# 64-wide attention of a fused two-layer kernel: the order of TensorE's work in slots 1, 4 and 12 of a round

## The reference, cut to what matters

```python
h = _rms(x, ln_w)
q = (h @ wq).reshape(B, S, NHEADS, HEAD_DIM)      # 32 heads of 64
k = (h @ wk).reshape(B, S, KVHEADS, HEAD_DIM)     # 8 groups
v = (h @ wv).reshape(B, S, KVHEADS, HEAD_DIM)
q, k = _rope(q, k)
scores = jnp.einsum('bqhd,bkhd->bhqk', q, k) / np.float32(np.sqrt(HEAD_DIM))
scores = jnp.where(causal[None, None], scores, jnp.float32(-1e+30))
attn = jax.nn.softmax(scores, -1)
o = jnp.einsum('bhqk,bkhd->bqhd', attn, v).reshape(B, S, NHEADS * HEAD_DIM)
x = x + o @ wo
```

## Time and profile before

| what | value |
|---|---|
| median of 3 runs | 2113.06 us (2111.1 to 2116.01) |
| the profiled execution, its own time | 2112.84 us |
| its span | 2111.0 us |
| mean granted TensorE clock | 0.935 of full speed |
| busy over the span | PE 86%, PEld 58%, DVE 63%, ACT 52%, POOL 43% |

### The profile page before, as it was taken

One profiled execution on the slowest core, in us unless ns is written; L12 is line 12 of the kernel. 1 busy time (PEld: TensorE's weight loads), 2 busy tenths in 40 slices (PEclk: granted clock), 3 DMA queues, 4 the chain that ended last, 5 costly groups with the idle time before them and its releaser, 6 DMA issues.

```text
span 2111.0 us, 32365 instructions
## 1 busy us (share of the span) xinstructions
PE 1810.6 (86%) x10666; PEld 1224.6 (58%) x10666; DVE 1320.8 (63%) x3898; ACT 1097.9 (52%) x2886; POOL 917.8 (43%) x1013
## 2 busy tenths in 40 slices
PE   4989899867888845999999999999999994799994
PEld 2656678733434323666666666666667664555552
DVE  5675545446686855777877777787777766522222
ACT  3323244226565533767666676666667661344441
POOL 3991000002221001555555555555555551588884
PEclk9999899958999986999999999999999995899997
DMA  5000020000001010000000000000000007255556
GB/s 152 1 1 2 1 60 1 1 0 1 1 1 41 1 43 1 1 1 1 1 1 1 1 1 1 1 1 1 1 1 1 1 1 276 73 82 84 82 84 163
DMA packets 61426, 61.71 MB, mean 29 GB/s; under 512 B 13136, under 2 KB 58320, under 8 KB 61264
## 3 DMA queue, kind: packets, MB, share of 16 engines
q0 software_dynamic: 15360, 20.98, 6.3%
q1 hardware_dynamic: 45904, 38.65, 5.7%
HBM read 40.48 MB, written 19.14 MB: 28 GB/s over the span
## 4 chain that ended last, share of the span: by engine, by line
PE 62%; DVE 21%; issue 8%; ACT 4%; POOL 3%; DMA 2%; SPq 0%; ACTq 0%; POOLq 0%; DVEq 0%
PE banks L1799 7%; PE banks L1818 6%; PE banks L1787 5%; PE banks L1777 5%; PE banks L1808 5%; DVE wide_x L1052 4%; PE banks L1995 3%; PE banks L1830 3%; PE banks L1621 3%; PE banks L1872 3%; PE banks L1847 2%; DVE con L1063 2%; POOL wdT L725 2%; PE banks L1683 2%; PE banks L1892 2%
## 5 line engine op out<-in xcount | busy, mean ns | idle before, releaser
L1777 PE MATMUL banks<-wide_k,wide_q 128*128 128x512 f32 (+3 forms) x1024 | 316.3, 391 | 7.2 <-DVE con L1033 3.9
L657 POOL TENSOR_TENSOR wugT<-wugT,con 128x512 f32<-128x512 f32 (+1 forms) x256 | 246.4, 984 | 5.1 <-DVE con L1016 2.1
L1406 ACT ACTIVATE wugT<-wugT,con 128x512 f32<-128x512 f32 (+1 forms) x256 | 169.9, 665 | 134.5 <-DVE con L1033 134.5
L1777 PEld LDWEIGHTS banks<-wide_k,wide_q 128*128 128x128 f32 x1024 | 167.1, 191 | 90.5 <-issue 35.8
L668 POOL TENSOR_TENSOR attn<-attn 128x320 f32<-128x320 f32 x128 | 111.4, 871 | 238.4 <-DVE attn L1004 238.4
L1033 DVE CUSTOM_DVE_ANT_0 wugT<-banks,wide_mask 128x512 f32<-128x512 f32 (+1 forms) x256 | 158.2, 618 | 86.1 <-PE banks L1777 82.7
L1063 DVE TENSOR_REDUCE con<-banks 128x1 f32<-128x512 f32 x256 | 163.6, 680 | 52.6 <-PE banks L1860 52.2
L1818 PE MATMUL banks<-late,xnT 128*128 128x384 f32 x512 | 192.1, 499 | 3.2 <-ACT xnT L1436 2.0
L1052 DVE TENSOR_TENSOR wide_x<-attn,wide_x 128x256 fp32r<-128x256 f32 (+1 forms) x256 | 174.1, 720 | 31.0 <-ACT wide_x L1440 31.0
L1799 PE MATMUL banks<-attn 128*64 128x256 f32 x1280 | 166.5, 389 | 0.0
L1995 PE MATMUL banks<-w,late 128*128 x320 | 156.5, 612 | 2.4 <-ACT late L1533 1.7
(11 more groups left out here) (311 smaller groups left out, 4191.0 us busy)
## 6 DMA issues: line engine op xcount, KB each, us to landing
w<-in_L_ffn_w_dram SPq DMA_DIRECT2D x32, 256.0 KB, 6.1
late<-in_L_ffn_w_dram SPq DMA_DIRECT2D x16, 256.0 KB, 6.2
y_rows<-wqkv1T SPq DMA_DIRECT2D x1, 2176.0 KB, 7.9
x<-in_L_attn_x_dram SPq DMA_DIRECT2D x4, 512.0 KB, 8.9
late<-in_L_ffn_wq_dram SPq DMA_DIRECT2D x2, 1024.0 KB, 7.3
late<-in_L_ffn_wo_dram SPq DMA_DIRECT2D x1, 2048.0 KB, 8.4
h_rows<-wugT SPq DMA_DIRECT2D x1, 2048.0 KB, 7.0
y_rows<-x SPq DMA_DIRECT2D x1, 2048.0 KB, 13.1
```

What stands on the lines that cost most here:

```text
L657: nc.gpsimd.tensor_tensor(p, p, rinv[:, m:m + 1].to_broadcast([P, n]), ALU.mult).then_inc(at.sem["norm"], 1)
L1406: nc.scalar.activation(at.prob(m)[:, 0:n], at.prob(m)[:, 0:n], ACT.Exp, bias=negmax[:, m:m + 1], scale=-1.0, accum_out=rowsum[:, m:m + 1]) ...
L1777: ins = nc.tensor.matmul(sbank[:, 0:keys], wide_q[:, side, i, qcols], wide_k[:, side, w, 0:keys], start=(w == 0), stop=(w == 1))
```

## The change

Three entries of the table move. In slot 1 and in slot 4, `qkv` of the next round comes ahead of `project` of the round before. In slot 12, `turn_qk` 4 of the next round comes behind `turn` 5 and the four `values`, as the last entry of its slot. Nothing else changes: no operation is added or taken away, and every operation keeps its shape. The bank of some `qkv` and `project` entries changes with the order, as `ybank` numbers them.

```diff
         WIDE = {0: [("stage", 1, 0), ("turn", -1, 8)],
-                1: [("project", -1, 1), ("qkv", 1, 0)],
+                1: [("qkv", 1, 0), ("project", -1, 1)],
                 2: [("values", -1, 7), ("values", -1, 8)],
                 3: [("high", 1, 0), ("turn", -1, 9)],
-                4: [("low", 1, 0), ("project", -1, 2), ("qkv", 1, 1)],
+                4: [("low", 1, 0), ("qkv", 1, 1), ("project", -1, 2)],
                 5: [("values", -1, 9)],
...
-                12: [("low", 1, 3), ("turn_qk", 1, 4), ("turn", 0, 5), ("values", 0, 0), ("values", 0, 1), ("values", 0, 2),
-                     ("values", 0, 3)],
+                12: [("low", 1, 3), ("turn", 0, 5), ("values", 0, 0), ("values", 0, 1), ("values", 0, 2), ("values", 0, 3),
+                     ("turn_qk", 1, 4)],
```

## The result

The changed kernel takes 2129.92 us (median of 7 runs, 2124.91 to 2135.16), against 2113.06 us before (7 runs, 2104.38 to 2116.01): ratio 1.0079, 95% interval 1.0058 to 1.0100, so 17 us slower. The profiled execution took 2126.39 us with a span of 2124.6; the mean granted clock is 0.939 of full speed.

A forecast was written before the change was run, and what follows sets the result against it. TensorE was taken as fullest, with 5% idle gaps from waits on VectorE and ScalarE. Per round 0.43 + 0 + 0.07 = 0.50 us, times 30 is 15.0, giving 2128.1 us; own range 2121 to 2136, 8-in-10 range 2110 to 2139.

The forecast's parts named there:

- The stall of `qkv` 0 for xnT: Slot 1: `qkv` 0, put first, waits for ScalarE's stage copy to xnT, 0.43 us a round.
- 1.85 again: Slot 1: the new pair takes 1.74 us plus 0.11 for starting behind a wait, the same 1.85 as the old.
- my upper bound of 0.55: Slot 1: cost a round if the new pair is no shorter than the old, against 0.43 forecast.
- That it all reaches the end: Slot 1's 0.43 us delays unit 4's scores, VectorE's chain behind them and so the end of the round.
- Slot 4, nothing: `qkv` 1 ahead of `project` 2: TensorE gains about 0.2 us, VectorE's sum to unit 5's maximum is unchanged; worth 0.
- Slot 12, +0.07: 0.94 us wait moves from `turn_qk` 4 to `turn_qk` 5, held by ScalarE's copy; +0.07 us a round, bounds -0.05 to +0.2.
- Sum: Whole round: 0.43 + 0 + 0.07 = 0.50 us in each of 30 steady rounds, 15.0 us.
- Nothing outside the rounds: Whole kernel: the forecast adds only the rounds' 15.0 us, with no term for the stretches before and behind them.
- A: Slot 12: the gap at `turn_qk` 4 is won, round changes by -0.51 us, 2098 us; chance 0.11.
- B: Slots 1 and 12: slack where TensorE waits for VectorE absorbs the 0.43, `turn_qk` neutral; 2113 to 2116 us; chance 0.11.
- C: VectorE's low parts lengthen by a GpSimd normalisation, up to 1.1 us a round; 2161 us, or 2145 with slack; chance 0.12.
- One sign that I had named: Profile after: `qkv` 0 idle some 0.4 us for xnT in 30 rounds, some 13 us in all.

The follow-up runs named there:

- the split copy: Changed kernel with ScalarE's copy to xnT in two instructions, the 128 tokens of `qkv` 0 first: 2115.03 us against 2114.87 before, ratio 1.0002.
- the swaps alone: Kernel before with `qkv` ahead of `project` in slots 1 and 4, `turn_qk` 4 unmoved: 2118.65 us, ratio 1.0018; second time 2124.94 us, ratio 1.0054.
- the move alone: Kernel before with only `turn_qk` 4 moved behind the four values in slot 12: 2116.24 us against 2114.87, ratio 1.0011.
- slot 1 alone: Kernel before with only slot 1 swapped, `qkv` 0 ahead of `project` 1: 2123.2 us against 2112.68, ratio 1.0052.
- slot 4 alone: Kernel before with only slot 4 swapped, `qkv` 1 ahead of `project` 2: 2113.09 us, ratio 0.9997.
- the other six kernels: The move alone; the split copy; slot 12 with two values or `turn` 5 ahead of `turn_qk` 4; `values` 9 in slot 4; two values plus that: 2082.24 to 2116.24 us.

## Why the prediction was right

The forecast of 2128.1 us came within 2 us of the median, and the chain of reasons held, with one term wrong in size and some luck outside the rounds.

- **The stall of `qkv` 0 for xnT, 0.43 us:** right, 0.97 - 0.55 = 0.42, shown by the split copy, which takes the whole of slot 1's loss away.
- **"1.85 again" for the pair:** this term was mis-sized. I credited the new order with 0.11 us, from `qkv` ahead of scores (0.99) and `project` ahead of scores (0.75), and set the start behind a wait (0.11) against it. The start does cost 0.11 (1.40 against 1.29). But there is no credit: `project` behind `qkv` starts 1.29 after it and not 0.99, and up to the `values` of slot 2 either order takes 3.26 us when nothing waits. So slot 1 costs 0.42 + 0.11 = 0.53, near my upper bound of 0.55, which was the case in which the new order wins nothing.
- **That it all reaches the end:** right. The stretch from the `values` of slot 2 to `project` 3 keeps its length (7.87, 7.86), and VectorE's chain moves as a whole (low part 0 to the maximum of unit 5: 3.12 us in both).
- **Slot 4, nothing:** right, to 0.1 us over the kernel. TensorE's gain of 0.23 was forecast too, at 0.2 to 0.3, but from the wrong source: the order gives nothing of it, the wait of `project` 2 that falls away gives all.
- **Slot 12, +0.07:** right. `turn_qk` 4 starts without a wait, unit 13's scores follow, and `turn_qk` 5 waits for ScalarE. ScalarE's run from the exponential of unit 11 to the end of the copy takes 2.73 us (1227.38 to 1230.11); I had 2.74. Measured +0.02 to `turn_qk` 5 and +0.05 behind it.
- **Sum:** 0.59 a round against 0.50, 16.9 us from first to last stage against 15.0. (2112.84 + 15.0 is 2127.84, not 2127.9, which changes nothing.)
- **Nothing outside the rounds:** this was taken without a reason, and that it held is luck. Behind the rounds the changed kernel takes 86.4 us where it was 85.8, but the kernel with the swaps alone takes 80.1. With such a stretch here the time would have come out some 6 us lower, by estimate from these two.
- **Rivals:** A fell with the move alone (no gain), B with slot 4 and with 16.9 us in the rounds, C with low parts of unchanged length (low part 0 takes 1.87 us and low part 2 1.38 in both). C's price, a whole normalisation and never a part, was read too strictly: in the kernel before, a normalisation of 0.61 us starts at 1223.09 and low part 3 at 1223.25; the first of its two instructions takes 0.74 us, and at most 0.45 of that, the rest of the normalisation, can be waiting.

One sign that I had named came otherwise: the wait of `qkv` sums to 7.2 us in the list and not 13, because idle time is counted only from the modelled end of the matmul before it (0.26 a time, where the stall is 0.42). `project` 3's wait stayed at 0.39 as said. The wait before unit 7's scores rose from 0.15 to 0.38, since slot 4's gain ends there.

## What to carry to other kernels

When an operation that waits is put further back, look at what stood behind it as cover: its result has a consumer too, and on a buffer of depth one the wait only changes its name. Divide the cover instead: put just enough work ahead of the operation to fill its gap, and leave the rest behind it. And measure a gap from start to start of the instructions around it, since idle time beside a matmul counts from a modelled end and shows less than the wait costs. Measure past the next group too: the price that an order seems to have at one start can be gone at the next.

## What the hardware showed unexpectedly

**The stretch behind the attention repeats for a kernel and differs between kernels.** From the last stage copy to the end of the scoring matmuls it takes 80.1 us in three profiles whose first to last stage is 898.2 us (both of the swaps and that of slot 1 alone), 85.8 in two at 882.7 (before, slot 4 alone) and 86.4 in two at 899.6 (both of the changed kernel), although the first stage starts anywhere from 800.4 to 808.9 us. In the other six kernels, one profile each, it takes 82.4 to 82.8 us (three of them) or 85.1 to 85.6, and neither value goes with long or short rounds. A difference of 1.4 us in the rounds (swaps against the whole change) thus comes with 6.3 more behind them, through a stretch at granted clock 1.00 or 0.50. The Trainium skill (TensorE: Matmul & The Clock Gate, "What's actually happening") says that the monitor behind the gate runs free of when a kernel starts. By that alone the stretch should vary between executions of the same kernel, and in these profiles, two each of two kernels, it does not. What ties it to the kernel no run here shows. For a change of this size it means that the rounds' own length in the trace says more than the time of the whole kernel.

**The order of two kinds of matmul costs nothing, though it seems to.** `project` and `qkv` one behind the other take 1.85 us from start to start in one order and 1.96 in the other (slot 1 of the kernel before and of the split copy), with the same instructions, no wait and the clock at 1.00. The scores behind them take 0.86 and 0.75 to the next start, and the sum from unit 1's scores to the `values` is 3.26 us in both.
